# The order of the groups in a routed two-layer kernel: four groups of the three-matrix class read last instead of fifth to eighth

## What is computed

```python
out_nr  = gelu(x @ w1_nr + b1_nr) @ w2_nr + b2_nr            # class 0
out_tsr = gelu(x @ w1_tsr + b1_tsr) @ w2_tsr + b2_tsr        # class 1
h = gelu(x @ w1_sr + b1_sr)                                  # class 2: 256 -> 512
h = gelu(h @ w2_sr + b2_sr)                                  #          512 -> 256
out_sr = h @ w3_sr + b3_sr                                   #          256 -> 256
x1 = layernorm(x + chosen) * gamma + beta
h = gelu(x1 @ down_W.T + down_b)                             # 256 -> 64
h = h @ expert_W[domain].T + expert_b[domain] + domain_emb[domain]
y = layernorm(h @ up_W.T + up_b + x1) * ln_gamma + ln_beta
```

## Time and profile before

| | us |
|---|---|
| median of 3 runs | 261.46 (261.38 to 261.81) |
| the profiled execution | 262.32 |
| its span | 260.5 |

### The profile page before, as it was taken

How to read it: one execution, slowest core, us unless ns; L and a number is a source line. 1 busy time by engine, 2 the same in 40 slices (tenths; PEclk the granted TensorE clock), 3 DMA queues, 4 the chain that set the end, 5 groups by cost and what they waited for, 6 DMA issues and landing times.

```text
span 260.5 us, 7556 instructions
## 1 busy us (share of the span) xinstructions
PE 241.2 (93%) x1881; PEld 235.9 (91%) x1881; DVE 211.5 (81%) x657; ACT 209.7 (81%) x554; POOL 159.0 (61%) x185
## 2 busy tenths in 40 slices
PE   7899998999999999999999999999999999998440
PEld 6799998899999999999999999999999999997320
DVE  5777776366675776799999999999999999998871
ACT  7877857658679779798999999999999989975510
POOL 4423740320262462687778878788878878768662
PEclk9979999999999999999999999999999999999755
DMA  6893232332332111222233233333233332322233
GB/s 192 303 326 107 76 93 81 95 88 79 93 87 60 41 45 43 62 66 71 66 85 66 71 86 83 76 73 88 63 83 84 67 83 51 68 54 43 63 74 77
DMA packets 23041, 22.86 MB, mean 88 GB/s; under 512 B 4785, under 2 KB 21875, under 8 KB 22976
## 3 DMA queue, kind: packets, MB, share of 16 engines
q1 hardware_dynamic: 22256, 21.32, 31.7%
q10 hardware_dynamic: 448, 0.35, 0.5%
q0 software_dynamic: 272, 0.38, 0.4%
HBM read 13.34 MB, written 8.65 MB: 84 GB/s over the span
## 4 chain that ended last, share of the span: by engine, by line
PE 83%; DVE 5%; ACT 3%; POOL 2%; issue 2%; DMA 1%; SPq 0%; DVEq 0%; ACTq 0%; POOLq 0%
PE ps_H L476 22%; PE ps_Y L580 19%; PE ps_Y L561 11%; PE ps_H L520 9%; PE ps_U L613 7%; PE ps_T L465 5%; PE ps_Z L591 3%; PE ps_H L386 2%; PE ps_Y L533 2%; DMA sb_xb<-in_x 1%; PE ps_U L434 1%; POOL sb_of L1099 1%; DVE sb_utab L1015 1%; POOL sb_of L1102 1%; DVE sb_hl L888 1%
## 5 line engine op out<-in xcount | busy, mean ns | idle before, releaser
L1099 POOL TENSOR_TENSOR sb_of<-sb_zf,sb_rows 128x512 f32<-128x512 f32 (+1 forms) x33 | 40.3, 1221 | 30.6 <-ACT sb_zf L728 29.4
L580 PE MATMUL ps_Y<-sb_wt,sb_hh 128*128 x264 | 58.6, 308 | 0.0
L476 PE MATMUL ps_H<-sb_xh,sb_w1h 128*128 128x256 f32 x168 | 50.5, 300 | 1.4 <-DVE sb_hl L888 1.4
L476 PE MATMUL ps_H<-sb_xh,sb_w1l 128*128 128x256 f32 x168 | 47.2, 281 | 0.0
L476 PE MATMUL ps_H<-sb_xl,sb_w1h 128*128 128x256 f32 x168 | 47.2, 281 | 0.0
L668 ACT ACTIVATE ps_H<-ps_H,sb_b1t 128x256 f32<-128x256 f32 x102 | 46.5, 455 | 0.0
L667 ACT ACTIVATE sb_hh<-ps_H,sb_b1t 128x256 fp32r<-128x256 f32 x66 | 31.3, 474 | 15.6 <-PE ps_H L520 15.6
L580 PEld LDWEIGHTS ps_Y<-sb_wt,sb_hh 128*128 128x128 f32 x264 | 43.1, 188 | 0.0
L1102 POOL TENSOR_TENSOR sb_of<-sb_of,sb_rows 128x512 f32<-128x512 f32 (+1 forms) x33 | 39.8, 1207 | 2.6
L728 ACT ACTIVATE sb_zf<-sb_x,sb_nb,sb_rs 128x256 f32<-128x256 f32 x61 | 33.7, 600 | 6.5 <-DVE sb_nb L954 5.3
L613 PE MATMUL ps_U<-sb_utab,sb_p 128*128 (+1 forms) x166 | 33.2, 305 | 3.5 <-DVE sb_p L928 3.5
(11 more groups left out here) (140 smaller groups left out, 638.3 us busy)
## 6 DMA issues: line engine op xcount, KB each, us to landing
out<-sb_of SPq DMA_DIRECT2D x132, 64.0 KB, 1.9
sb_xb<-in_x SPq DMA_DIRECT2D x130, 64.0 KB, 2.2
sb_xb<-in_w SPq DMA_DIRECT2D x2, 512.0 KB, 6.7
sb_xb<-in_w SPq DMA_DIRECT2D x1, 768.0 KB, 6.2
sb_xb<-in_w2t SPq DMA_DIRECT2D x1, 768.0 KB, 6.8
sb_xb<-in_we SPq DMA_DIRECT2D x1, 576.0 KB, 4.4
sb_xb<-in_w SPq DMA_DIRECT2D x2, 256.0 KB, 6.7
sb_rows<-in_rows SPq DMA_DIRECT2D x1, 384.0 KB, 7.4
```

Source lines behind the costliest of these rows:

```text
L476: last = pe.matmul(o, w1ap(wa, c, kc, m), xa[:, g % 3, kc, :], start=(k == 0), stop=(k == 5))
L580: last = pe.matmul(psY[t][:, 0:D + A], ha[:, g % 2, kc, 128 * t:128 * t + 128], wt[:, bass.ds(c, 1), i, kc, :], start=False, stop=(k == 5) ...
L1099: pool.tensor_tensor(of[:, g % 2, ts, :], zf[:, g % 2, ts, :], rws[:, 1, None, :].to_broadcast(bc), ALU.mult).then_inc(q2, 1)
```

## The change

Places 0 to 3 and 32 to 34 read the sorted group of their own number as before. Places 4 to 27 read sorted groups 8 to 31, and places 28 to 31 read sorted groups 4 to 7. Every read of `ri` and `rc` goes through the function `sorted_group`. With the inputs here, places 0 to 4 are SR, 5 to 27 light, 28 to 31 SR, and 32 light.

```diff
+FRONT, BACK = 4, 4
...
+def sorted_group(g):
+    return FRONT + (g - FRONT + BACK) % (NGMIN - FRONT) if FRONT <= g < NGMIN else g
...
-                    self.quads[q] = self.load(rc[2:3, 4 * q:min(4 * (q + 1), NG)], 0, 3)
+                    self.quads[q] = self.load(rc[2:3, sorted_group(4 * q):min(sorted_group(4 * q) + 4, NG)], 0, 3)
...
-                    return self.load(ri[r:r + 1, G * g:G * g + G], 0, NB + r * NS - 1)
+                    lo = G * sorted_group(g)
+                    return self.load(ri[r:r + 1, lo:lo + G], 0, NB + r * NS - 1)
...
-                    lo = 2 * G * (g // 2)
+                    lo = G * sorted_group(2 * (g // 2))
...
-                    regs.tabs = regs.load(ri[3:4, 4 * h:4 * h + 4], 0, NV - 1)
+                    regs.tabs = regs.load(ri[3:4, G * sorted_group(h):G * sorted_group(h) + G], 0, NV - 1)
...
-                    v = regs.load(ri[3:4, 4 * g + 2 * t:4 * g + 2 * t + 2], 0, NV - 1)
+                    lo = G * sorted_group(g) + 2 * t
+                    v = regs.load(ri[3:4, lo:lo + 2], 0, NV - 1)
```

## The result

The changed kernel takes 280.92 us in the median (278.55 to 281.46, 4 runs), beside 261.63 for the kernel before; the ratio is 1.0684, with a 95% interval of 1.0644 to 1.0723. I had forecast 272.8 with a range of 270.6 to 276.5: the direction was right, the size was not, 19 us instead of 11. The profiled execution has a span of 279.6 us, 19.1 more than before.

A forecast was written before the change was run, and what follows sets the result against it. TensorE, busy 93% of the span, was taken as the bound until VectorE sets the drain's pace. Seams +0.2, Gsr stall +11.5 and drain -0.4 add 11.3 to the median 261.46, giving 272.8 us, range 270.6 to 276.5.

The forecast's parts named there:

- TensorE is full in both kinds of place, so the permutation gives nothing: TensorE works 58.08 of 58.55 us in SR places, 27.33 of 27.33 in light; reordering the same groups changes 0 but for seams.
- Gsr ahead of AB holds XP back by 2.87 us at each of four places: Places 28 to 31: AB queued behind Gsr on ScalarE, XP starts 5.79 us behind L1 instead of 2.92; +11.5 us in all.
- four waits of 2.7 to 3.1 us: Sign to look for: TensorE waits for AB before XP at places 28 to 31, none elsewhere beyond the one of 1.0.
- I take no fall, because full work surrounds each gap for 9 us: TensorE's granted clock stays at 1.00 through the 2.9 us gaps at four places, up to the drain; adds 0.
- The rival that had this case at 14%: The stall at the four places comes with falls of TensorE's clock: 274.8 to 280.8 us; chance 14%.
- A fall costs up to 2 us: One clock fall lasts about a 6.5 us slice, losing 2 us at most; 274.8 with one, 280.8 in all four places.
- The Trainium skill: Page cited for TensorE's clock: by its rule the gaps could each send XP, HP and part of L2 to half clock.
- Loads and stores, 0: SyncE keeps its order, and light places starting four places earlier ask no more DMA per place; 0 us.
- The seams, +0.2: SR to light seam, where XP takes 0.25 us more, stands twice (4 to 5, 31 to 32) instead of once; +0.2, 0 to 0.6.
- The drain, -0.4: From L1 of place 32 on, HT and G2 come up to 0.6 us earlier; -0.4 us, between -1.4 and 0.
- Runs of this kernel lie 0.43 us apart: Spread of the kernel's runs, taken to mean about 0.2% can be told from no change.

The follow-up runs named there:

- e1: Changed kernel with ScalarE's late shift of Gsr (-0.419) removed; 263.35 us against 263.06 for the kernel before, ratio 1.0008.
- e2: Changed kernel, shift kept, with 20 unread matmuls put into TensorE's wait ahead of XP of places 27 to 30; 275.35 us, ratio 1.0430 to the kernel before.
- e4: Kernel before, its order of groups unchanged, with the -0.419 shift given to Gsr of places 4 to 7; 280.46 us, ratio 1.0646.
- e11: e1 with 24 places loaded ahead of the first store instead of 22; 270.57 us, ratio 1.0291 to the kernel before.
- e12: Kernel before with 24 places loaded ahead of the first store instead of 22; 263.25 us, ratio 0.9983.
- e5: Changed kernel with the late shift of Gsr at -0.3, behind G2 and ahead of both AB; 275.87 us, ratio 1.0501 to the kernel before.
- e3: e1 with 14 places loaded ahead of the first store instead of 22, then one place per store instead of per two; 283.97 us, ratio 1.0748.
- e6: Changed kernel with the late shift of Gsr at -0.2, between AB of tile 0 and AB of tile 1; 270.59 us.

## Why the prediction was wrong, point by point

- **TensorE is full in both kinds of place, so the permutation gives nothing**: right, and shown by e1, which is level with the kernel before.
- **Gsr ahead of AB holds XP back by 2.87 us at each of four places**: right in mechanism and size. XP came 5.78 us behind L1 (5.79 forecast), e2 puts the term at 11.4 to 12.0 us (11.5), and e4 has the same waits in the old order of the groups. A small part of the fit is luck: in e1 XP of the same places starts 3.06 us behind L1 in the mean and not 2.92, so the shift moves it by 2.72, and the rest of the 2.85 a place comes behind XP. The sign that the text gave, four waits of 2.7 to 3.1 us, came short: they were 2.56 to 2.58.
- **"I take no fall, because full work surrounds each gap for 9 us"**: this is the step that failed, 5.7 us. The sum had put this term at nothing. Three of the four gaps of 2.56 us (and all four of 2.55 to 2.62 in e4) brought the clock to 0.50, with 9 us and more of dense matmuls on either side, and e2 takes exactly this part away: 275.35 us with the waits kept and the clock up, which is inside the stated range. The evidence against the step stood in the text: the gap lay nearer to the 3.48 us with a fall than to the 1.00 us without one. I overruled the nearer row with an argument for which no row spoke. The rival that had this case at 14% gave 274.8 to 280.8; two of the four executions lie in it (278.55 and 280.56) and two just above (281.28 and 281.46).
- **A fall costs up to 2 us**: this held roughly and not fully. The three falls cost 1.5, 2.7 and 1.5 us (each place against its own in e2). The text took its 2 us from one slice of the page; the fall at place 30 cost more than that by itself.
- **The Trainium skill** ("TensorE: Matmul & The Clock Gate", Part 1: the throttled state is the default, activity releases it) pointed the right way; e2, which adds nothing but activity, agrees with it, by 5.7 us.
- **Loads and stores, 0**: right on average and wrong on the cover. That "a light stretch that starts four places earlier asks for no more DMA per place" holds for the rate, but the first store leaves near 78 us in both kernels (78.39 and 78.48), behind the loads queued ahead of it, and the light places now reach it. e11 and e12 show that the class 2 places 5 to 8 were the cover: 7.2 us against 0.
- **The seams, +0.2**: right at the first (XP 1.6 us behind L1 in both kernels), too little at the second, where XP came 1.97 us behind L1 at place 32 instead of 1.41, 0.6 us.
- **The drain, -0.4**: wrong in sign. From L1 of place 32 it took 29.65 us in the changed kernel and in e1, against 29.2. The late seam accounts for all of that: the last F starts 22.68 to 22.71 us behind this L1 in three profiles of the old order without a fill in the drain, and 23.23 to 23.29 in seven of the new. The earlier HT did come (the last G2 at 15.53 us behind L1, against 15.46, although EX was 0.6 us late), but F does not wait for it.
- **"Runs of this kernel lie 0.43 us apart"**: three runs were too few to say so. A fourth was 263.55, and the 23 runs on another chip go from 261.42 to 264.64. The size of the change makes this harmless for the verdict.

## What to carry to other kernels

A shift in a table that no input has exercised still takes effect once one does: before data are put in another order, read the list that each engine will run at the new places, and ask of each wait what is queued behind it. When a change opens a gap in TensorE, price the gap twice, once for the wait and once for the matmuls that run behind it at half clock; here the second was half of the first, and 20 unread matmuls in each gap bought it back. A queue whose first stores stand behind a fixed list of loads has to be checked against the earliest user in the new order, not only against its rate.

## What the runs showed of the hardware

- The granted clock fell behind seven of eight gaps of 2.55 to 2.62 us (three of four in the changed kernel, four of four in e4), behind two of the four of 1.83 to 1.88 us in e5, and behind single gaps of 3.09 us in e3 and 4.62 in e11. It stayed up behind all four gaps of 1.35 to 1.40 us in e6 and behind gaps of 1.30, 1.32, 1.47 and 1.61 us in e3. All of them had dense matmuls on both sides.
- Executions of one program differ in it: of e5 one took 273.77 us at a mean granted clock of 0.956, another 277.31 at 0.944. Those of e2, with the gaps filled, lie 2.2 us apart, at 0.966 to 0.971.
- The three falls of the changed kernel cost 1.5, 2.7 and 1.5 us, the one of e11 some 1.6.
- SyncE issues a 64 KB transfer in 0.63 us (four in 2.52 to 2.54 at the fastest). Four loads and four stores with their register loads and waits took some 6.3 us, which is over the 5.47 us that a light place takes.
- What stays open: which of two equal gaps is followed by a fall. The rows around them do not tell them apart.
